# Where the recurrence's first estimates of h and x are kept: a change to a fused RNN, attention and feed-forward kernel

## The chip, the cores and the metric

The kernel runs on one core of one Trainium2 chip. Its time is the device time of one execution in microseconds; of the kernel before there are three runs without a profile (3483.38, 3485.22 and 3495.51 us, median 3485.22) and one execution with a profile. The engines are called as in the profile: PE is TensorE's matmul, PEld its weight load, DVE is VectorE, ACT is ScalarE, POOL is GpSimd, SP is SyncE. PSUM is eight banks of 512 fp32 numbers per partition; POOL cannot reach it.

## What is computed

The input is x of shape (8, 128, 128) and a condition of shape (8, 128). A recurrence of 128 steps comes first; a latent attention, a gated scan and six layers of local attention and feed-forward follow on its result. All is fp32. The change lies in the recurrence, which is

```python
xw = jnp.einsum('ntd,dh->nth', x, Wx) + b
def step(prev_h, xw_t):
    next_h = jnp.tanh(xw_t + prev_h @ Wh)
    return (next_h, next_h)
_, hs = jax.lax.scan(step, h0, jnp.swapaxes(xw, 0, 1))
```

with 8 sequences, a state of 128 numbers each, and h0 the condition. The rest of the program follows from `hs`.

## The kernel before

**One step.** The kernel forms `prev_h @ Wh` and `x_t @ Wx` not as one matmul each but as sums in a fixed order, number by number. For each of the 8 sequences (a "row" n here) and each output, it first needs the running sums over the 128 products. They come from a matmul of the weights with a triangle (the state times the matrix `upto`), 128 running sums per row; kept with 12 added or taken away (`OFFSET`) they are the *guess*. The error of each link is the *rest*: the guess shifted by one place, minus the guess itself, plus the exact product, and the product is built of four products of parts, upper and lower half of the weight's bits (`w_part`) times upper and lower half of the value (a diagonal matrix, `diag`), in fp32r. Rests, guesses and minus the guesses are laid side by side in one chain (`adds`, three numbers per link: rest, guess, minus guess; it lies in the tile `qkv_w`), and a sum over the chain (`fold`, L993, one instruction for 1 to 3 rows before) gives the row's result. The state's `tanh` follows on DVE as some forty small instructions and ends in `h_made`; `open_step` copies it (`h_now`, L969) and prepares the next step.

**Halves.** The 8 rows go in two halves of four rows; a half's sums fill one PSUM bank of 4 x 128. h's sums lie in banks 0 and 1, x's in bank 4. h's rests go in quarters of two rows (banks 2, 3, 0, 1), x's rests in halves through bank 6. x runs one step ahead: in step t the kernel makes x's sums and rests for t + 1.

**Who does what.** PE: the sums (L1355, L1303), identity matmuls that bring the difference of guesses into the rests' bank (L1322 for h; L1331 and, with minus the identity, L1332 for x), the products (L1298). ACT: the guess (`take_sums`, L705, PSUM to SBUF; h's guess in the tile `w1`, x's in `b1`), the diagonals of x (L698) and six of h's lower ones (L693), and the copies of the rests into the chain (`place_rests`, L716). DVE: h's difference of guesses (`difference_h`, L987, SBUF minus SBUF), the folds, the upper diagonals of h's first half (L980), `tanh`. POOL: the second half's triangle of h and both of x (L572), the upper diagonals of h's second half, the last lower ones, and the copies of guess and minus guess into the chain (`place_sums`, L581 and L583).

**What sets the order.** Each engine has its own program, written out by hand, with one loop over the 128 steps; an engine takes its instructions strictly in the order written, and semaphores with counts (`wait_ge`) tie the engines together. There is no planner. A wait therefore also holds all that is written behind it. The semaphores that matter: `sum_ready` (sums in PSUM), `guessed`, `diff_ready`, `split_h` (h's upper and lower parts), `rest_ready` (rests in PSUM), `rest_placed` and `sum_placed` (in the chain), `x_scanned` (x's folds done, so its chain may be overwritten).

## Time and profile before

| | |
|---|---|
| runs without a profile | 3483.38, 3485.22, 3495.51 us |
| the profiled execution | 3494.39 us, span 3492.2 us |
| granted TensorE clock over the span | 0.982 |
| busy, share of the span | PE 84%, DVE 83%, POOL 75%, ACT 69%, PEld 57% |
| instructions | 60815 |
| recurrence, 43 to 2150 us | 2107 us |

The span is the time from the first to the last instruction; the execution's own time lies 2.2 us around it. The busy share is a mean over the recurrence (43 to 2150 us), the latent attention and gate, and the layers, which have different limits. In the recurrence all steps look alike, so one step can stand for all. In a timeline row equal instructions that follow each other without a pause are merged; the second number is from the first start to the last end, and a bracket shows how long the engine stood idle before it and whose instruction ended that. Starts of successive instructions lie closer than their durations, since each overlaps the next a little; fp32 matmuls are recorded as two passes each.

### The profile page before, as it was taken

What the parts mean: (1) busy time and instruction counts of PE and PEld (TensorE: products, weight loads), DVE (VectorE), ACT (ScalarE), POOL (GpSimd) and SP (SyncE); (2) the same over time, 40 slices, a digit from 0 to 9 for tenths busy, and PEclk for the clock granted to TensorE, in tenths of its full rate; (3) what the DMA queues carried; (4) which work ended last, traced back from release to release, by engine and by line L of the source; (5) the groups of instructions that cost most, each with busy time, mean ns of one, the idle gap of its engine ahead of it and who ended that gap; (6) DMA issues with size and microseconds to landing.
All of it is one profiled execution on the core that took longest, in us unless ns stands there. A gap on an engine that the chain in (4) does not pass through costs nothing.

```text
span 3492.2 us, 60815 instructions
## 1 busy us (share of the span) xinstructions
PE 2949.2 (84%) x14887; PEld 2000.2 (57%) x14887; DVE 2899.3 (83%) x8319; ACT 2393.0 (69%) x5656; POOL 2607.6 (75%) x2800
## 2 busy tenths in 40 slices
PE   5888888888888888888888888978999999999997
PEld 3445445445545544544554555765777677777776
DVE  5999999999999999999999997336777877777775
ACT  5777777777777777777777775336666666666665
POOL 7888888888888887888888885008778777787773
PEclk9999999999999999999999998879999999999998
DMA  1000000000000000000000002000010101000000
GB/s 32 0 0 0 0 0 0 0 0 0 0 0 0 0 0 0 0 0 0 0 0 0 0 0 70 1 1 1 0 35 0 35 0 35 0 3 31 0 0 7
DMA packets 21861, 21.97 MB, mean 6 GB/s; under 512 B 6335, under 2 KB 19397, under 8 KB 21061
## 3 DMA queue, kind: packets, MB, share of 16 engines
q1 hardware_dynamic: 21828, 21.55, 1.9%
q8 instruction: 20, 0.33, 0.0%
q14 instruction: 13, 0.10, 0.0%
HBM read 21.02 MB, written 0.52 MB: 6 GB/s over the span
## 4 chain that ended last, share of the span: by engine, by line
PE 54%; DVE 16%; ACT 15%; issue 10%; POOL 3%; ACTq 1%; DVEq 0%; SPq 0%; DMA 0%; POOLq 0%
PE bank L1298 13%; PE bank L1322 8%; PE bank L1331 7%; PE bank L1332 6%; ACT diag_x L698 6%; ACT qkv_w L716 4%; PE bank L1303 3%; DVE rot_s L1211 3%; DVE qk L987 3%; PE bank L1549 3%; ACT w L705 2%; DVE rot_c L1211 2%; DVE ss L1214 2%; PE bank L1627 2%; PE bank L1601 2%
## 5 line engine op out<-in xcount | busy, mean ns | idle before, releaser
L993 DVE TENSOR_REDUCE bank<-qkv_w 128x2 f32<-128x766 f32 (+2 forms) x1024 | 925.3, 946 | 28.8 <-ACT qkv_w L716 28.8
L716 ACT COPY qkv_w<-bank 128x256 f32<-128x256 f32 (+1 forms) x770 | 480.0, 623 | 550.3 <-PE bank L1298 547.3
L698 ACT ACTIVATE diag_x<-eye,X 128x128 fp32r<-128x128 f32 x2072 | 630.5, 390 | 0.0
L1298 PE MATMUL bank<-diag_h,w_part 128*128 128x256 f32 x2048 | 495.5, 354 | 0.0
L581 POOL TENSOR_TENSOR qkv_w<-w,offset 128x512 f32<-128x512 f32 x256 | 331.3, 1294 | 156.8 <-ACT w L705 156.8
L1322 PE MATMUL bank<-qk,eye 128*128 128x256 f32 x1024 | 331.1, 405 | 98.0 <-DVE qk L987 98.0
L651 POOL TENSOR_TENSOR qk<-rot_c,rot_s 128x512 f32<-128x512 f32 x192 | 256.5, 1336 | 209.4 <-DVE rot_s L1211 209.4
L1331 PE MATMUL bank<-b,eye 128*128 128x512 f32 x516 | 277.8, 620 | 128.8 <-ACT qkv_w L716 128.8
L1298 PE MATMUL bank<-diag_x,w_part 128*128 128x512 f32 x1032 | 386.0, 495 | 0.0
L1298 PEld LDWEIGHTS bank<-diag_h,w_part 128*128 128x128 f32 x2048 | 335.0, 190 | 88.3 <-issue 61.2
L581 POOL TENSOR_TENSOR qkv_w<-b,offset 128x512 f32<-128x512 f32 x258 | 269.0, 1043 | 89.4 <-DVE bank L993 75.4
L658 POOL TENSOR_TENSOR rs<-rs,halfs 128x8 f32<-128x8 f32 x192 | 320.1, 1667 | 16.0
L987 DVE TENSOR_TENSOR qk<-w 128x512 f32<-128x512 f32 x256 | 225.3, 880 | 116.8 <-ACT w L705 116.8
L1549 PE MATMUL bank<-qkv_w,xsT 128*128 (+1 forms) x576 | 310.7, 622 | 8.8 <-DVE rot_s L1211 7.3
L1355 PE MATMUL bank<-qT,wh 128*128 128x256 f32 x512 | 144.6, 405 | 168.4 <-DVE qT L972 168.4
L583 POOL TENSOR_SCALAR qkv_w<-w 128x512 f32<-128x512 f32 x256 | 273.2, 1067 | 17.3
L1303 PE MATMUL bank<-kT,wx 128*128 128x512 f32 x516 | 265.6, 596 | 16.8 <-POOL kT L572 16.0
L1298 PEld LDWEIGHTS bank<-diag_x,w_part 128*128 128x128 f32 x1032 | 195.0, 189 | 147.2 <-issue 123.9
L572 POOL TENSOR_TENSOR kT<-upto,xT 128x512 f32<-128x512 f32 x260 | 265.0, 1040 | 10.3
L1332 PE MATMUL bank<-b,qk 128*128 128x512 f32 x516 | 264.3, 594 | 0.0
L693 ACT ACTIVATE diag_h<-eye,part 128x128 fp32r<-128x128 f32 x768 | 250.4, 394 | 0.0
L583 POOL TENSOR_SCALAR qkv_w<-b 128x512 f32<-128x512 f32 x258 | 229.2, 888 | 17.5
(235 smaller groups left out, 6883.8 us busy)
## 6 DMA issues: line engine op xcount, KB each, us to landing
qkv_w<-in_L_ffn_Wqkv SPq DMA_DIRECT2D x6, 1536.0 KB
o_w<-in_L_ffn_Wo SPq DMA_DIRECT2D x6, 512.0 KB
w<-in_L_ffn_W SPq DMA_DIRECT2D x6, 341.0 KB
b<-in_L_ffn_b SPq DMA_DIRECT2D x6, 341.0 KB
w<-in_L_ffn_W SPq DMA_DIRECT2D x6, 128.0 KB
x_tok<-in_x SPq DMA_DIRECT2D x1, 512.0 KB
masks<-in_masks SPq DMA_DIRECT2D x1, 512.0 KB, 3.5
out<-o_fin SPq DMA_DIRECT2D x1, 512.0 KB, 3.2
```

Source lines behind the costliest of these rows:

```text
L581: pool.tensor_tensor(adds[n][:, rows, :, 1], src, offset[:, 0:1].unsqueeze(2).to_broadcast([P, 4, D]), ALU.add)
L583: ins = pool.tensor_scalar(adds[n][:, rows, :, 2], src, -1.0, OFFSET, ALU.mult, ALU.add)
L698: ins = act.activation(diag[1][:, d, m, :], eye[:], ACT.Copy, scale=scale)
L716: act.copy(adds[n][:, rows, :, 0], src).then_inc(rest_placed[n], 1)
L987: dve.tensor_tensor(diff_h[:, rows, :], guess[0][:, rows, 0:D], guess[0][:, rows, 1:], ALU.subtract).then_inc(diff_ready, 1)
L993: return dve.tensor_reduce((sum_h, sum_x)[n][:, a:b], chain[n][:, a:b, 0:LINKS], AX_X, ALU.add)
L1298: return pe.matmul(dst, w_part[:, n, w], diag[n][:, d, a:b, :].rearrange("p n k -> p (n k)"), start=start, stop=stop)
L1303: pe.matmul(bank[:, SUM_BANK_X if n else half, :], (wh, wx)[n][:], tri[n][:, 4 * half:4 * half + 4, :].rearrange("p n k -> p (n k)"), star ...
L1322: pe.matmul(bank[:, bnk, 0:(b - a) * D], eye[:], diff_h[:, a:b, :].rearrange("p n k -> p (n k)"), start=False, stop=False)
L1331: pe.matmul(rows, eye[:], guess[1][:, a:b, 0:D], start=True, stop=False)
L1332: pe.matmul(rows, minus_eye, guess[1][:, a:b, 1:], start=False, stop=False)
L1549: pe.matmul(bank[:, c % 2, :], xsT[:, par, :], w[:, at:at + BANK], start=True, stop=True).then_inc(qkv_ready, 1)
```

## The change

h's sums now start from a bank that PE has filled with 12 by a small bf16 matmul of a row of ones with a row of twelves (`offset_h`, two banks per step), and are added onto it; so the guess is what stands in PSUM, and it is not copied to SBUF as such. ACT writes it, less 12, straight into the chain (`place_guess_h`), and later minus the guess for the first half (`place_minus_h`); POOL writes minus the guess for the second half from the chain. DVE forms the difference from the PSUM bank (shifted by one) and the chain's guess and writes it into the rests' bank (`difference_h`), where PE adds the products: h's identity matmuls go. h's rests are now in halves (banks 2 and 3), each product 512 wide.

For x, ACT writes minus the guess into the rests' bank (`less_guess_x`), and PE adds the shifted guess with one identity matmul; the one with minus the identity goes. x's lower diagonals move from ACT to POOL, h's upper diagonals of the first half from DVE to POOL, all of h's lower ones of the second half to POOL (of the first half: ACT). x's folds are two of four rows, one before and one behind both differences. One matmul per rests' bank is added ahead of the loop.

```diff
+            def offset_h():
+                for half in range(2):
+                    pe.matmul(bank[:, half, :], offset16[:, 0:D], offset16[:, D:], start=True, stop=True,
+                              skip_group_check=True)
 ...
             def rests_x(half, count):
-                pe.wait_ge(guessed[1], count)
-                pe.matmul(rows, eye[:], guess[1][:, a:b, 0:D], start=True, stop=False)
-                pe.matmul(rows, minus_eye, guess[1][:, a:b, 1:], start=False, stop=False)
-                pe.wait_ge(diag_x_ready, count)
-                times(at, 1, 0, 0, a, b, False, False)
-                other_products(1, REST_BANK_X, a, b)
+                pe.wait_ge(less_guess, count)
+                pe.matmul(rows, eye[:], guess_x[:, a:b, 0:D], start=False, stop=True, skip_group_check=True)
+                for d in range(2):
+                    pe.wait_ge(diag_x_ready[d], count)
+                    times(at, 1, 0, d, a, b, False, False)
+                    ins = times(at, 1, 1, d, a, b, False, d == 1)
+                ins.then_inc(rest_ready[1], 1)
 ...
+            def less_guess_x(half):
+                act.activation(bank[:, REST_BANK_X, :], guess_x[:, 4 * half:4 * half + 4, 1:], ACT.Copy,
+                               scale=-1.0).then_inc(less_guess, 1)
+            def place_guess_h(half, count):
+                act.wait_ge(sum_ready[0], count)
+                act.activation(adds[0][:, 4 * half:4 * half + 4, :, 1], bank[:, half, :].rearrange("p (n k) -> p n k", k=D),
+                               ACT.Identity, bias=offset[:, 0:1], scale=1.0).then_inc(guess_placed, 1)
+            def place_minus_h(count):
+                act.wait_ge(diff_ready, count)
+                act.activation(adds[0][:, 0:4, :, 2], bank[:, 0, :].rearrange("p (n k) -> p n k", k=D),
+                               ACT.Identity, bias=offset[:, 1:2], scale=-1.0).then_inc(minus_placed[0], 1)
 ...
-            def difference_h(half, halves):
-                rows = slice(4 * half, 4 * half + 4)
-                dve.wait_ge(guessed[0], halves)
-                dve.tensor_tensor(diff_h[:, rows, :],
-                                  guess[0][:, rows, 0:D], guess[0][:, rows, 1:],
-                                  ALU.subtract).then_inc(diff_ready, 1)
+            def difference_h(half, count):
+                sums_ = bank[:, half, :].rearrange("p (n k) -> p n k", k=D)
+                dst = bank[:, REST_BANKS_H[half], :].rearrange("p (n k) -> p n k", k=D)
+                placed = adds[0][:, 4 * half:4 * half + 4, :, 1]
+                dve.wait_ge(guess_placed, count)
+                dve.tensor_scalar(dst[:, :, 0:1], sums_[:, :, 0:1], -1.0, OFFSET, ALU.mult, ALU.add)
+                dve.scalar_tensor_tensor(out=dst[:, :, 1:], in0=sums_[:, :, 0:D - 1], scalar=-OFFSET, in1=placed[:, :, 1:],
+                                         op0=ALU.add, op1=ALU.subtract).then_inc(diff_ready, 1)
 ...
+                pool.wait_ge(split_h, this)
+                for half in range(2):
+                    diagonal(0, 0, half, part[:, 0, 4 * half:4 * half + 4], diag_upper_h)
+                pool.tensor_copy(hT[:, bass.ds(t, 1), :].rearrange("p a n -> p (a n)"), h_now[:]).then_inc(h_ready, 1)
+                diagonal(0, 1, 1, part[:, 1, 4:8], diag_lower_h[1])
+                pool.wait_ge(guess_placed, counts[1])
+                pool.tensor_tensor(adds[0][:, 4:8, :, 2], adds[0][:, 4:8, :, 1],
+                                   signs[:, 1:2].unsqueeze(2).to_broadcast([P, 4, D]), ALU.mult).then_inc(minus_placed[1], 1)
+                pool.wait_ge(rest_ready[1], counts[1])
+                diagonal(1, 1, 1, lower_x(around, 1), diag_x_ready[1])
                 pool.wait_ge(x_scanned, this)
+                place_sums_x(0, counts[2])
+                place_sums_x(1, counts[3])
+                pool.wait_ge(rest_ready[1], counts[2])
+                diagonal(1, 1, 0, lower_x(beyond, 0), diag_x_ready[1])
                 for half in range(2):
                     triangle(1, at_step(value(pool, t + 2)), half, tri_x)
```

The instructions' order shows three places. First ACT from the start of the loop body; `w` is h's guess before, `b` x's guess, `qkv_w` the chain. Before:

```order
L693 ACTIVATE diag_h<-eye,part 128x128 [waits split_h]
L693 ACTIVATE diag_h<-eye,part 128x128
L704 ISA
L705 ACTIVATE w<-bank,offset 128x4x128 [waits sum_h]
L704 REGISTER_ALU
L705 ACTIVATE w<-bank,offset 128x4x128 [waits sum_h]
L693 ACTIVATE diag_h<-eye,part 128x128 x4
L704 REGISTER_ALU [waits sum_placed_x]
L705 ACTIVATE b<-bank,offset 128x4x128 [waits sum_x]
L713 ISA
L716 COPY qkv_w<-bank 128x256 [waits rest_h]
L713 REGISTER_ALU
```

After (L735 is the guess into the chain, L741 minus the guess, L753 the rests, L728 x's guess, L723 minus the guess into PSUM):

```order
L735 ACTIVATE qkv_w<-bank,offset 128x512 [waits sum_h]
L777 REGISTER_ALU
L712 ACTIVATE diag_h<-eye,part 128x128 [waits split_h]
L712 ACTIVATE diag_h<-eye,part 128x128 x3
L741 ACTIVATE qkv_w<-bank,offset 128x512 [waits diff_h]
L753 COPY qkv_w<-bank 128x256 [waits rest_h]
L753 COPY qkv_w<-bank 128x256
L727 REGISTER_ALU [waits sum_placed_x]
L728 ACTIVATE b<-bank,offset 128x4x128 [waits sum_x]
L723 ACTIVATE bank<-b 128x512 [waits rest_placed_x,guessed_x]
L753 COPY qkv_w<-bank 128x256 [waits rest_h]
L753 COPY qkv_w<-bank 128x256
```

h's guess stood behind two diagonals of h; two writes into the chain now come first, of which the first stands just ahead of this piece, all four diagonals behind them, and x's guess and its minus stand between the second and the third copy of h's rests.

PE from h's products on; `qk` is the tile of h's difference before. Before:

```order
L1298 MATMUL bank<-diag_h,w_part 128x256 [waits diag_upper_h]
L1298 MATMUL bank<-diag_h,w_part 128x256
L1373 ISA [waits diff_h]
L1322 MATMUL bank<-qk,eye 128x256 [waits diag_lower_h]
L1298 MATMUL bank<-diag_h,w_part 128x256 x3
L1373 REGISTER_ALU
L1322 MATMUL bank<-qk,eye 128x256 [waits diag_lower_h]
L1298 MATMUL bank<-diag_h,w_part 128x256 x3
L1298 MATMUL bank<-diag_h,w_part 128x256 [waits guessed_h,diag_second_h]
L1298 MATMUL bank<-diag_h,w_part 128x256
```

After:

```order
L1340 MATMUL bank<-diag_h,w_part 128x512 [waits diag_upper_h,diff_h]
L1340 MATMUL bank<-diag_h,w_part 128x512
L1340 MATMUL bank<-diag_h,w_part 128x512 [waits diag_upper_h,diff_h]
L1340 MATMUL bank<-diag_h,w_part 128x512
L1340 MATMUL bank<-diag_h,w_part 128x512 [waits diag_lower_h0]
L1340 MATMUL bank<-diag_h,w_part 128x512
L1340 MATMUL bank<-diag_h,w_part 128x512 [waits diag_lower_h1]
L1340 MATMUL bank<-diag_h,w_part 128x512
L1344 REGISTER_ALU [waits guessed_x]
L1345 MATMUL bank<-kT,wx 128x512 [waits tri_x]
L1364 MATMUL bank<-b,eye 128x512 [waits less_guess_x,rest_placed_x]
```

The identity matmuls (L1322) are gone, the products are twice as wide and half as many; both halves' upper products come ahead of the lower ones, and x's identity matmul (L1364) waits for ACT's write into the bank.

DVE from x's first fold on. Before:

```order
L993 TENSOR_REDUCE bank<-qkv_w 128x2 [waits sum_placed_x,rest_placed_x]
L986 REGISTER_ALU
L987 TENSOR_TENSOR qk<-w 128x512 [waits guessed_h]
L993 TENSOR_REDUCE bank<-qkv_w 128x1
L987 TENSOR_TENSOR qk<-w 128x512 [waits guessed_h]
L993 TENSOR_REDUCE bank<-qkv_w 128x3
L1096 ISA
L993 TENSOR_REDUCE bank<-qkv_w 128x2 [waits sum_placed_h,rest_placed_h]
```

After:

```order
L1035 TENSOR_REDUCE bank<-qkv_w 128x4 [waits sum_placed_x,rest_placed_x]
L1029 TENSOR_SCALAR bank<-bank 128x4 [waits guess_placed_h]
L1030 SCALAR_TENSOR_TENSOR bank<-bank,qkv_w 128x4x127
L1028 REGISTER_ALU
L1029 TENSOR_SCALAR bank<-bank 128x4 [waits guess_placed_h]
L1030 SCALAR_TENSOR_TENSOR bank<-bank,qkv_w 128x4x127
L1035 TENSOR_REDUCE bank<-qkv_w 128x4 [waits sum_placed_x,rest_placed_x]
L1138 ISA
L1140 REGISTER_ALU [waits rest_placed_h]
L1035 TENSOR_REDUCE bank<-qkv_w 128x2 [waits minus_placed_h0]
```

The four rows of x that were split over three folds around the differences now stand as one fold ahead of them, and x's last rows, which came behind h's fourth row, ahead of h's first; each difference is two instructions, of which the first writes four numbers.

## Rows read from the trace of the kernel before

**Rows 1.** The page: busy time, share, instructions; granted clock in 40 slices.
```profile
PE 2949.2 (84%) x14887; PEld 2000.2 (57%) x14887; DVE 2899.3 (83%) x8319; ACT 2393.0 (69%) x5656; POOL 2607.6 (75%) x2800
...
PEclk9999999999999999999999998879999999999998
```

**Rows 2.** Busy time by stretch; this one is the recurrence.
```profile
43.00:2150.00 2107.00, 1712.07 (x6394) 1060.86 (x6393) 1967.77 (x6649) 1563.22 (x4093) 1708.61 (x1789) 1.00 0.00 0
```

**Rows 3.** Waits in the recurrence: total us, times, longest us.
```profile
ACT qkv_w L716 <- PE bank L1298: 534.0, 505, 3.0
...
DVE qk L987 <- ACT w L705: 114.3, 127, 1.7
```

**Rows 4.** Timeline of ScalarE, one step: start us, us, instruction, count, idle before.
```profile
1013.77 0.83 ACT L716 COPY qkv_w<-bank 128x512 f32<-128x512 f32 x1 [3.00 <-PE bank L1298]
1014.45 2.43 ACT L698 ACTIVATE diag_x<-eye,X 128x128 fp32r<-128x128 f32 x8
1016.79 0.68 ACT L693 ACTIVATE diag_h<-eye,part 128x128 fp32r<-128x128 f32 x2
1017.37 1.24 ACT L705 ACTIVATE w<-bank,offset 128x512 f32<-128x512 f32 x2
...
1030.23 0.83 ACT L716 COPY qkv_w<-bank 128x512 f32<-128x512 f32 x1 [3.00 <-PE bank L1298]
```

**Rows 5.** Timeline of VectorE in the same step.
```profile
1014.52 0.17 DVE L969 COPY h_now<-bank 128x8 f32<-128x8 f32 x1
...
1015.54 0.68 DVE L980 TENSOR_TENSOR diag_h<-eye,bank 128x512 fp32r<-128x512 f32 x1
1016.23 0.96 DVE L993 TENSOR_REDUCE bank<-qkv_w 128x2 f32<-128x766 f32 x1
1018.08 0.69 DVE L987 TENSOR_TENSOR qk<-w 128x512 f32<-128x512 f32 x1 [0.89 <-ACT w L705]
...
1020.14 4.77 DVE L993 TENSOR_REDUCE bank<-qkv_w 128x3 f32<-128x1149 f32 x5
...
1024.96 0.94 DVE L993 TENSOR_REDUCE bank<-qkv_w 128x2 f32<-128x766 f32 x1
```

**Rows 6.** Timeline of TensorE in the same step.
```profile
1015.07 1.13 PE L1355 MATMUL bank<-qT,wh 128*128 128x256 f32 x4 [1.34 <-DVE qT L972]
...
1027.28 1.13 PE L1331 MATMUL bank<-b,eye 128*128 128x512 f32 x2 [1.00 <-ACT qkv_w L716]
1028.24 1.02 PE L1332 MATMUL bank<-b,qk 128*128 128x512 f32 x2
1028.70 1.49 PE L1298 MATMUL bank<-diag_x,w_part 128*128 128x512 f32 x4
```

**Rows 7.** Groups by line and form: busy us, mean ns, idle before.
```profile
L993 DVE TENSOR_REDUCE bank<-qkv_w 128x3 f32<-128x1149 f32 x128 | 172.1, 1345 | 0.0
...
L1017 DVE TENSOR_TENSOR_SCAN bank<-bank,f_add 128x96 f32<-128x96 f32 x128 | 45.3, 354 | 0.0
...
L716 ACT COPY qkv_w<-bank 128x256 f32<-128x256 f32 x512 | 262.0, 512 | 133.0 <-PE bank L1298 130.0
...
L716 ACT COPY qkv_w<-bank 128x512 f32<-128x512 f32 x258 | 218.0, 845 | 417.3 <-PE bank L1298 417.3
...
L705 ACT ACTIVATE w<-bank,offset 128x512 f32<-128x512 f32 x256 | 159.2, 672 | 0.0
...
L854 ACT COPY probT<-bank 128x512 f32<-128x512 f32 x192 | 102.9, 594 | 1.8 <-PE bank L1397 1.8
...
L572 POOL TENSOR_TENSOR kT<-upto,xT 128x512 f32<-128x512 f32 x260 | 265.0, 1040 | 10.3
```

**Rows 8.** Line L928: duration ns min/median/max, first and last start.
```profile
L928 DVE COPY xT<-bank x1: 1078/1078/1078, 6.8 to 6.8; 128x512 f32<-128x512 f32 x1
```

**Rows 9.** TensorE's timeline in the layers.
```profile
2410.14 0.33 PE L1658 MATMUL bank<-eye,xn 128*128 128x128 f32 x1 [1.90 <-DVE xn L1274]
```

**Rows 10.** Busy time by stretch just after, PEclk the granted clock.
```profile
2412.00:2419.00 7.00, 6.47 (x30) 4.36 (x31) 6.40 (x9) 2.24 (x4) 5.09 (x5) 0.52 0.01 2
```

More of the change, by code:

```diff
@@ L263, in program @@
         quot_part = sb("quot_part", [P, NB, 2])
-        clamped, rc, q0, nq, small_x, h_upper = (own(0, NB) for _ in range(6))
+        clamped, rc, q0, nq, small_x = (own(0, NB) for _ in range(5))
         q_tmp = sb("q_tmp", [P, 4, NB])
@@ L536, in _ @@
                     pool.memset(rest_seq[:, 3 * block_ + r::9, 3:4], c_low)
-            for n in range(2):
-                ins = pool.memset(guess[n][:, :, 0:1], OFFSET)
-            ins.then_inc(rnn_const, 1)
+            pool.memset(guess_x[:, :, 0:1], OFFSET).then_inc(rnn_const, 1)
             pool.memset(wd[:], 0.0)
@@ L599, in _ @@
                 counts = [value(pool, two + n) for n in (1, 2, 3, 4)]
+                around, beyond = (value(pool, (t + n) % T) for n in (1, 2))
                 pool.wait_ge(h_static, this)
@@ L702, in take_sums, with lower_h @@
-            def take_sums(n, half, count):
-                act.wait_ge(sum_ready[n], count)
-                act.activation(guess[n][:, 4 * half:4 * half + 4, 1:],
-                               bank[:, SUM_BANK_X if n else half, :].rearrange("p (n k) -> p n k", k=D), ACT.Identity,
-                               bias=offset[:, 1:2], scale=1.0).then_inc(guessed[n], 1)
-            def place_rests(n, counts, first, last):
-                rows_ = NB // len(counts)
-                for m in range(first, last):
-                    act.wait_ge(rest_ready[n], counts[m])
-                    rows = slice(rows_ * m, rows_ * m + rows_)
-                    src = bank[:, REST_BANK_X if n else REST_BANKS_H[m], 0:rows_ * D].rearrange("p (n i) -> p n i", n=rows_)
-                    act.copy(adds[n][:, rows, :, 0], src).then_inc(rest_placed[n], 1)
+            def lower_h():
+                for n in range(4):
+                    ins = act.activation(diag[0][:, 1, n, :], eye[:], ACT.Copy, scale=part[:, 1, n:n + 1])
+                ins.then_inc(diag_lower_h[0], 1)
@@ L718, in _, with place_rests_h @@
+            def place_rests_h(half, count):
+                act.wait_ge(rest_ready[0], count)
+                for m in range(2):
+                    rows = slice(4 * half + 2 * m, 4 * half + 2 * m + 2)
+                    act.copy(adds[0][:, rows, :, 0],
+                             bank[:, REST_BANKS_H[half], 2 * m * D:2 * m * D + 2 * D].rearrange(
+                                 "p (n i) -> p n i", i=D)).then_inc(rest_placed[0], 1)
             act.wait_ge(in_x, 64)
@@ L1097, in placed_h @@
                     if m % 2 == 0:
-                        dve.wait_ge(sum_placed[0], counts[m // 2])
+                        dve.wait_ge(minus_placed[m // 2], this)
                 dve.sem_clear(rnn_op)
+                placed_x(counts[0])
+                fold(1, 0, 4)
+                for half in range(2):
+                    difference_h(half, counts[half])
                 placed_x(counts[1])
-                for half in range(2):
-                    fold(1, *X_SCAN[half])
-                    difference_h(half, counts[half])
-                fold(1, *X_SCAN[2])
+                fold(1, 4, 8).then_inc(x_scanned, 1)
                 placed_h(0)
@@ L1109, in _ @@
                 fold(0, 2, 4)
-                fold(1, *X_SCAN[3]).then_inc(x_scanned, 1)
+                dve.wait_ge(x_scanned, this)
+                step(dve.tensor_scalar(xw[:], sum_x, rnn_b[:], None, ALU.add))
                 placed_h(2)
                 fold(0, 4, 6)
-                dve.wait_ge(x_scanned, this)
-                step(dve.tensor_scalar(xw[:], sum_x, rnn_b[:], None, ALU.add))
                 placed_h(3)
```

204 lines of the change are left out of this document (103 added, 101 removed).

## The prediction

> **What bounds the kernel now.** I read the page first, for busy shares and clock. PE and DVE are both busy over 80% of the span and the clock is at 2.4 GHz nearly throughout [rows 1], so neither names the bound. The sum by stages comes next: the recurrence takes 2107 of 3492 us, and the change touches nothing else but a few setup instructions [rows 2]. In it DVE is busy 1968 us, PE 1712, POOL 1709, ACT 1563; no one is full. The list of waits shows who stands still: ACT waits 534 us for PE's rests and DVE 114 us for h's guess [rows 3].
>
> So the timeline of one step has to be followed, from h_now at 1014.52. The period is the distance of equal rows: 1013.77 to 1030.23 on ACT, 16.46 us [rows 4]; 128 of them are 2107 us, the whole stage. What the reader is to see is a ring through ACT's queue. PE ends x's second rests [rows 6], ACT copies them (1013.77), must then write eight diagonals of x (2.43 us) and two of h, and only at 1017.37 does it turn h's first sums into the guess, although PE had begun those sums at 1015.07 and they last 1.13 us [rows 4, 6]. DVE idles 0.89 us for it, subtracts at 1018.08 and from there has no gap until the last fold at 1024.96 [rows 5]. PE starts x's second rests at 1027.28 after ACT's copy of the first and needs 1.02 us for each fp32 matmul (spaced 0.86, as 1027.28, 1028.24 and 1028.70 show with the 0.1 of a restart), then 1.49 for four products [rows 6], and the ring closes at 1030.23. Behind it runs a second ring, DVE's own: it is 1.1 us shorter, since the sums are ready at about 1016.20 and the guess is begun 1.17 later. Whoever shortens the first ring by more meets DVE.
>
> **The change, part by part, in us per step after h_now.** The stretch from the last fold to the next h_now is not touched: 16.46 - 10.44 = 6.02 us (10.44 is 1024.96 - 1014.52) [rows 5]. So the question is when the last fold starts.
>
> First ring. For x, four diagonals instead of eight stand on ACT in each group (2.43 for eight of them is 0.29 apart [rows 4], so 1.17 less), the two minus-identity matmuls leave PE (2 x 0.86), and x's second copy now comes last in ACT's step with nothing between it and h's sums. Placed one after the other (with the times found below: h's fourth copy done at 8.97, x's guess to 9.54, four diagonals to 10.71, x's first copy 0.85, minus the guess 0.75 with its waits, PE 0.10 + 0.86 + 0.94 + 0.16, to 14.37, x's second copy 0.85) it ends at 15.2 to 15.3, and h's next sums are ready 1.7 after the next h_now: this ring has some 2 us of room and no longer bounds.
>
> DVE's ring. *Start.* diag_h leaves DVE (0.68 [rows 5]) and goes to POOL. What stands behind it is the loop's turn (branch, semaphore clear), which it covered. Bounds 0 and 0.68; I take 0.06, first fold at 1.65 instead of 1.71, because the loop's turn is also in the queue. *Fold of four rows of x.* Three rows last 1.345, two 0.96, so 0.40 per row; spaced 1.66 [rows 5, 7]: to 3.31. The guess of the first half is placed by then: sums 1.7, ACT's strided write 0.67 + 0.25 = 0.92 (the contiguous form is 0.672, and a copy into the same every-third-number layout costs 0.845 against 0.594 [rows 7]) gives 2.65. So DVE's wait of 0.89 is gone; 0.66 of cover is left.
>
> *The two subtractions,* now PSUM minus SBUF into PSUM, one number in three read from the chain. No row shows one. Lower bound: the present subtraction, 0.69 [rows 5]. Upper bound: the scan, 0.354 for 96 numbers; less 0.15 fixed (h_now's eight numbers last 0.17) 2.1 ns each, so 508 take 1.23 [rows 5, 7]. In between lies the stride: ACT's 0.25 extra over 512 is 0.5 ns per number, hence 1.32 instead of 0.83, and 1.32 x 512 + 0.15 = 0.83; a DVE copy that writes every eighth number lasts 1.078 [rows 7, 8]. I take 0.83, spaced 0.75, since ACT's layout is this one. With a small instruction of 0.08 ahead of each, the second ends at 3.31 + 0.08 + 0.75 + 0.08 + 0.83 = 5.05.
>
> The Trainium skill (SBUF — State Buffer, under "Door 1: The DMA port swizzle") has a rule that speaks against this edit: accesses in the same 16-byte line run at full speed, each crossing pays, so every third fp32 pays on most numbers. The trace agrees for writes (0.845 against 0.594); no row shows a read. If reads pay as writes do, the sum stands; if not, the subtraction is 0.69 and the time 35 us lower.
>
> *PE.* Upper products of the second half, then the lower ones of the first: the four products of rows 6 run 0.23 apart (from 1028.24 + 0.86 to 1030.19, less 0.16 until the last is written), so 0.05 + 4 x 0.235 + 0.17: rest 1 is ready at 6.20. The identity matmuls for h and 16 products of 256 are replaced by eight of 512, the same 1.9 us; the fp32 identity (0.43 x 4) is gone from the path. *ACT behind it:* two copies of 256 (0.37 apart), x's guess (0.57, 0.15 more until it may read its own result), minus the guess into PSUM, then the third copy, 0.51 [rows 7]. ACT writing PSUM has no row: bounds 0.59 (contiguous copy) and 1.07 (strided by eight) for its duration; I take 0.65, 0.55 apart, nearest the contiguous rows, as both sides are contiguous. 6.25 + 0.74 + 0.72 + 0.55 + 0.51 = 8.77. DVE is ready for the third h fold at 4.96 + 1.66 = 6.62, waits for the first copy until 6.80, then 2 x 0.86 + 0.13 = 8.65, waits to 8.80, and begins the last fold at 9.66.
>
> *Sum:* 10.44 - 9.66 = 0.78 earlier, 128 times: 100 us. The new period is 15.68. x's pipeline ends before the next h_now, on ACT at 15.3 and on POOL at 14.9 (from x's first guess at 7.7 seven writes of at most 1.04 [rows 7]; in all thirteen and a small copy, near the 1709 / 128 = 13.35 of now [rows 2]): hidden; if POOL's cover goes, each step grows by what it overruns, as its first job is h's second triangle. The hT copy and the lower diagonal now stand behind two diagonals of POOL instead of one, and the second half's minus copy behind them; of these the diagonal is ready at 4.5 and asked for by PE at 6.0, the minus copy at 5.5 and asked for by DVE at 8.7. The other new waits are reached after their event: ACT's minus copy (behind it the copies of the rests) at 4.6, the first subtraction ends at 4.2; POOL's last x diagonal (behind it the triangles) at 11.9, the rests are ready at 10.6; PE's offsets at 10.4, the minus copy is done at 5.5. The two offset matmuls (0.44) lie between x's rests, where PE waits. Setup: three more fp32 matmuls (2.6 us) and two more POOL diagonals (2.0) before the first step, eight ACT diagonals less: +2. The profiled execution took 3494.4 for a span of 3492.2, so it would be 3396; it is 9 above the median of the runs, 3485.2, and against that the forecast is 3387.
>
> **Rivals.** *A, the stride costs as much as in the DVE copy, 1.07 [rows 8].* Two subtractions each 0.24 later and a PE restart: +0.58, period 16.25, 3460. For it: that row is DVE's own. Against: it strides by eight, not three.
>
> *B, slower: the fused two-operation subtraction out of and into PSUM runs far below one number per cycle.* Place: both instructions on DVE, everything behind them. The gain of 0.78 pays for 2 x 0.34 beyond 0.83, so the point is 1.2 us each. At 1.5 the last fold starts at 9.66 + 1.34 + 0.1 = 11.1, period 17.1, 3570. For it: the scan's 2.1 ns, which gives 1.23 with no stride. Against: the triangle and the diagonal, PSUM times SBUF, run at 1.05 ns (0.68 for 512 [rows 5]).
>
> *C, the clock.* PE loses 3.0 us of work per step net and gains a pause: from 14.4 to 16.2, 1.9 us, where before it was about 1.3 (last product to 1015.07) at a held 2.4 GHz. In the layers a pause of 1.90 before 2410.14 was followed by a stretch with a granted clock of 0.52, that is 1.2 GHz mostly [rows 9, 10]. If the products behind the subtraction run at 1.2 GHz in every step, 0.94 is added: period 16.6, 3505. Against: there the matmuls around were narrow, here they are full. In most phases only the sums are hit, and 0.66 covers them: +0.2, 3410. The Trainium skill (TensorE: Matmul & The Clock Gate, under "A second HAM failure mode: psum-queue depth-cycling") says that short idles between groups can make the clock swing; the trace shows swings in the layers and none in the recurrence. By it the time would be this rival's.
>
> *D, ACT's write to PSUM costs 1.0:* +0.35, one to one, as it stands before the third copy: 3432. I count it with the forecast.
>
> **How the numbers follow.** Forecast with D 0.56, range of its own 3345 to 3435 (unstrided subtraction to D); A 0.15; B 0.15; C at its worst 0.08; another wait that eats the gain 0.06, half of it within 0.5%. A measurement of this kernel tells about 0.5% from no change, 17 us, so 3468 and 3503 are the limits. Faster: 0.56 and 0.14 of A = 0.70; within: 0.01 of A, 0.02 of B, 0.03 of C, 0.03 of the last = 0.09; slower: 0.13 of B, 0.05 of C, 0.03 of the last = 0.21. The range 3345 to 3500 leaves out B and the tail of C above, little below.
>
> **What would show it.** Period 15.7 between equal ACT rows; no DVE gap ahead of the first subtraction; each 0.8 us; DVE gaps of 0.1 to 0.2 ahead of the first and third h fold, released by ACT's copies; POOL's writes all 1.04; ACT idle ahead of h's first sums, where it was full; granted clock 1.0 in the recurrence. It would be wrong with a subtraction over 1.0, a row of minus the guess near 1.0, a clock below 1.0 there, or POOL reaching h's triangle late.

## The result and the profile after

| | before | after |
|---|---|---|
| four runs, median (range) | 3484.4 us (3483.38 to 3495.51) | 3387.68 us (3386.6 to 3388.72) |
| ratio after to before, 95% interval | | 0.9715 (0.9695 to 0.9735) |
| profiled execution, span | 3494.39, 3492.2 us | 3387.04, 3385.2 us |
| one step of the recurrence | 16.46 us | 15.67 us |

The forecast was 3387, with a range of 3345 to 3500. The fourth run of the kernel before, 3483.58, was taken beside those of the changed kernel, whose four runs include the profiled one. In all periods below, a step is the distance between two copies to h_now, as a mean over the recurrence without its first step.

The page after, which answers to [rows 1], and the busy time by stretch, which answers to [rows 2]. The columns of the second are PE, PEld, DVE, ACT, POOL, then the granted clock:

```profile
PE 2591.3 (77%) x12477; PEld 1621.5 (48%) x12587; DVE 2810.1 (83%) x8061; ACT 2325.5 (69%) x4750; POOL 2593.7 (77%) x2804
...
PEclk9999999999999999999999998979999999999998
```

```profile
43.00:2050.00 2007.00, 1371.79 (x4097) 686.64 (x4096) 1879.51 (x6399) 1500.44 (x3205) 1693.84 (x1793) 1.00 0.00 0
```

The share of DVE is 83% on both pages, and the kernel is 97 us faster: a busy share says nothing here, since work and waiting fell together. DVE's busy time is 1967.77 of 2107 us before and 1879.51 of 2007 after, that is 15.37 and 14.67 us per step. In the list of waits of the recurrence the 114 us for h's guess [rows 3] are gone, 0.90 per step; two others stand there, 0.76 together:

```profile
DVE bank L1035 <- issue: 64.9, 127, 0.6
...
DVE bank L1035 <- ACT qkv_w L753: 31.9, 127, 0.3
```

By this account most of the gain looks like work taken off DVE, above all the diagonal of 0.68. The run a_hdve below shows that it is not.

ScalarE's timeline, one step, against [rows 4]. L735 is h's guess into the chain, L741 minus the guess, L753 the copies of h's rests, L746 those of x's:

```profile
1012.34 0.85 ACT L746 COPY qkv_w<-bank 128x512 f32<-128x512 f32 x1 [1.01 <-PE bank L1340]
1015.24 1.81 ACT L735 ACTIVATE qkv_w<-bank,offset 128x512 f32<-128x512 f32 x2 [2.06 <-PE bank L1355]
1016.89 1.25 ACT L712 ACTIVATE diag_h<-eye,part 128x128 fp32r<-128x128 f32 x4
1018.04 0.94 ACT L741 ACTIVATE qkv_w<-bank,offset 128x512 f32<-128x512 f32 x1
1019.82 0.84 ACT L753 COPY qkv_w<-bank 128x256 f32<-128x256 f32 x2 [0.84 <-PE bank L1340]
...
1021.21 0.60 ACT L723 ACTIVATE bank<-b 128x512 f32<-128x512 f32 x1
1021.75 0.88 ACT L753 COPY qkv_w<-bank 128x256 f32<-128x256 f32 x2
...
1028.01 0.84 ACT L746 COPY qkv_w<-bank 128x512 f32<-128x512 f32 x1 [1.01 <-PE bank L1340]
```

Where ACT was full between x's last copy and h's guess, it now stands idle for 2.06 us: the first ring no longer bounds. VectorE in the same step, against [rows 5]; h_now is at 1013.52:

```profile
1013.52 0.17 DVE L1013 COPY h_now<-bank 128x8 f32<-128x8 f32 x1
...
1015.14 1.76 DVE L1035 TENSOR_REDUCE bank<-qkv_w 128x4 f32<-128x1532 f32 x1 [0.51 <-issue]
1016.80 0.16 DVE L1029 TENSOR_SCALAR bank<-bank 128x4 f32<-128x4 f32 x1
1016.87 0.84 DVE L1030 SCALAR_TENSOR_TENSOR bank<-bank,qkv_w 128x508 f32<-128x508 f32 x1
1017.61 0.17 DVE L1029 TENSOR_SCALAR bank<-bank 128x4 f32<-128x4 f32 x1
1017.68 0.85 DVE L1030 SCALAR_TENSOR_TENSOR bank<-bank,qkv_w 128x508 f32<-128x508 f32 x1
1018.43 1.75 DVE L1035 TENSOR_REDUCE bank<-qkv_w 128x4 f32<-128x1532 f32 x1
1020.44 1.82 DVE L1035 TENSOR_REDUCE bank<-qkv_w 128x2 f32<-128x766 f32 x2 [0.25 <-ACT qkv_w L753]
```

No wait stands ahead of the first subtraction. Two small ones are new: 0.51 ahead of x's first fold, which no instruction of another engine ends ("issue"), and 0.25 for ACT's copy of h's rests. TensorE's pause ahead of h's sums, against [rows 6]:

```profile
1026.48 1.50 PE L1340 MATMUL bank<-diag_x,w_part 128*128 128x512 f32 x4
1029.75 1.56 PE L1355 MATMUL bank<-qT,wh 128*128 128x256 f32 x5 [1.77 <-DVE qT L1016]
```

### The profile page after: what moved, and what is told of

It reads as the page before. It is cut to its first block, busy times and chain, and to the rows that moved or that the text cites. A ratio compares the mean times of both kernels' runs of the same rounds, so it can differ in the third digit from the quotient of the medians.

```text
span 3385.2 us, 53537 instructions
## 1 busy us (share of the span) xinstructions
PE 2591.3 (77%) x12477; PEld 1621.5 (48%) x12587; DVE 2810.1 (83%) x8061; ACT 2325.5 (69%) x4750; POOL 2593.7 (77%) x2804
## 4 chain that ended last, share of the span: by engine, by line
DVE 53%; PE 21%; issue 16%; ACT 4%; POOL 3%; DVEq 2%; SPq 0%; DMA 0%; POOLq 0%; ACTq 0%
DVE bank L1035 12%; PE bank L1340 5%; DVE bank L1030 3%; DVE bank L1007 3%; DVE rot_s L1253 3%; DVE sq L1007 3%; DVE rot_c L1253 3%; DVE ss L1256 3%; PE bank L1582 2%; DVE qT L1016 2%; PE bank L1660 2%; DVE fix_trace L1101 2%; PE bank L1444 2%; PE bank L1634 2%; ACT qkv_w L753 2%
## 5 line engine op out<-in xcount | busy, mean ns | idle before, releaser
L1035 DVE TENSOR_REDUCE bank<-qkv_w 128x2 f32<-128x766 f32 (+1 forms) x768 | 914.0, 1220 | 123.6 <-issue 64.9
L1355 PE MATMUL bank<-qT,wh 128*128 128x256 f32 (+1 forms) x768 | 254.6, 467 | 224.0 <-DVE qT L1016 224.0
L669 POOL TENSOR_TENSOR qk<-rot_c,rot_s 128x512 f32<-128x512 f32 x192 | 256.9, 1338 | 207.8 <-DVE rot_s L1253 207.8
L735 ACT ACTIVATE qkv_w<-bank,offset 128x512 f32<-128x512 f32 x256 | 232.0, 960 | 261.1 <-PE bank L1355 261.1
L1340 PE MATMUL bank<-diag_h,w_part 128*128 128x512 f32 x1024 | 307.4, 422 | 118.1 <-DVE bank L1030 106.9
L587 POOL TENSOR_TENSOR diag_h<-eye,part 128x512 fp32r<-128x512 f32 x384 | 394.0, 1040 | 0.0
L1364 PE MATMUL bank<-b,eye 128*128 128x512 f32 x516 | 273.3, 611 | 156.7 <-ACT bank L723 156.7
L718 ACT ACTIVATE diag_x<-eye,X 128x128 fp32r<-128x128 f32 x1036 | 328.0, 389 | 0.3 <-DVE X L1128 0.3
L1340 PEld LDWEIGHTS bank<-diag_h,w_part 128*128 128x128 f32 x1024 | 172.7, 188 | 302.8 <-DVE bank L1030 279.8
L746 ACT COPY qkv_w<-bank 128x512 f32<-128x512 f32 x258 | 217.3, 842 | 134.6 <-PE bank L1340 133.4
L753 ACT COPY qkv_w<-bank 128x256 f32<-128x256 f32 x512 | 218.4, 508 | 104.3 <-PE bank L1340 104.3
L587 POOL TENSOR_TENSOR diag_x<-eye,X 128x512 fp32r<-128x512 f32 x259 | 269.7, 1041 | 10.2
```

The lines of the kernel that those rows point to most:

```text
L587: pool.tensor_tensor(diag[n][:, d, rows, :], eye[:].unsqueeze(1).to_broadcast([P, 4, D]), values.unsqueeze(2).to_broadcast([P, 4, D]), ALU ...
L718: ins = act.activation(diag[1][:, 0, m, :], eye[:], ACT.Copy, scale=scale)
L753: act.copy(adds[0][:, rows, :, 0], bank[:, REST_BANKS_H[half], 2 * m * D:2 * m * D + 2 * D].rearrange("p (n i) -> p n i", i=D)).then_inc(r ...
L1035: return dve.tensor_reduce((sum_h, sum_x)[n][:, a:b], chain[n][:, a:b, 0:LINKS], AX_X, ALU.add)
L1340: return pe.matmul(dst, w_part[:, n, w], diag[n][:, d, a:b, :].rearrange("p n k -> p (n k)"), start=start, stop=True, skip_group_check=True)
L1355: return pe.matmul(bank[:, half, (a - 4 * half) * D:(b - 4 * half) * D], wh[:], tri[0][:, a:b, :].rearrange("p n k -> p (n k)"), start=Fal ...
```

## The experiments

The kernel before was run again beside each group of experiments; its medians lie between 3484 and 3489 us, and each ratio is to the one taken beside the run. b_psum and a_contig compute with other numbers than the right ones (said with each): they measure a cost and are not kernels to be used.

| run | us, median | ratio to before, 95% | step, us |
|---|---|---|---|
| before | 3484 to 3489 | | 16.46 |
| after | 3387.7 | 0.9695 to 0.9735 | 15.67 |
| b_swap | 3431.3 | 0.9817 to 0.9853 | 16.03 |
| b_psum | 3311.2 | 0.9475 to 0.9506 | 15.07 |
| a_xboth | 3383.9 | 0.969 to 0.9725 | 15.65 |
| a_hdve | 3394.2 | 0.9714 to 0.9746 | 15.74 |
| a_contig | 3346.5 | 0.9571 to 0.9609 | 15.36 |
| a_order | 3375.0 | 0.9657 to 0.969 | 15.61 |
| o_mm | 3333.7 | 0.955 to 0.9603 | 15.31 |
| a_rot | 3318.8 | 0.9496 to 0.9531 | 15.15 |
| f_mm | 3275.6 | 0.937 to 0.9401 | 14.81 |
| f_both | 3277.2 | 0.9371 to 0.941 | 14.81 |
| h1_flat | 3262.8 | 0.9343 to 0.9392 | 14.72 |
| h2_late | 3239.6 | 0.9275 to 0.9301 | 14.47 |

**b_swap: was it ACT's order alone?** On the kernel before:

```diff
-                place_rests(1, counts[2:4], 0, 2)
+                place_rests(1, counts[2:4], 0, 1)
                 diagonals_x(beyond, 0, 0)
                 diagonals_x(beyond, 0, 1)
+                place_rests(1, counts[2:4], 1, 2)
```

> The kernel before, with one edit: ACT writes x's eight diagonals for the next group ahead of x's second copy of the rests, while it would wait 3.0 us for PE anyway. My theory: the bound was ACT's order alone, 2.43 us of diagonals between the copy and h's first guess; with them in ACT's pause DVE no longer waits 0.89 for the guess, DVE's own ring (1968 us of work in 128 steps, 15.4 each) takes over, period 15.5 to 15.6 instead of 16.46, time 3365 to 3380, as much as the whole change gave (3388). Rival one: what counted is the work taken off ACT and PE for x (four diagonals, the minus-identity matmul); the order alone then only shifts the wait to x's second copy, which stands ahead of h's diagonals still, gain under 0.3 per step, 3450 or more. Rival two: PE's pause ahead of h's sums grows and its clock falls: 3450 to 3500 and a granted clock under 1.0 in the recurrence.

Measured 3431, period 16.03: a gain of 0.43 per step where 0.86 to 0.96 was expected. DVE's wait for the guess is gone, as expected, but its two differences (L988 here) have grown, and so has a write of POOL. The two engines' timelines:

```profile
1022.95 1.50 DVE L988 TENSOR_TENSOR qk<-w 128x512 f32<-128x512 f32 x1
...
1024.83 0.81 DVE L988 TENSOR_TENSOR qk<-w 128x512 f32<-128x512 f32 x1
```

```profile
1022.86 1.04 POOL L581 TENSOR_TENSOR qkv_w<-w,offset 128x512 f32<-128x512 f32 x1
1023.97 1.24 POOL L583 TENSOR_SCALAR qkv_w<-w 128x512 f32<-128x512 f32 x1
```

POOL's first write ends at 1023.90, the difference that started beside it at 1024.45, 0.55 later, as if most of its 0.69 had only begun then. POOL's next write, 0.90 elsewhere, lasts 1.24. The second rival is out (the clock is 1.00 in the recurrence), and the first put the time at 3450 or more, with a gain under 0.3; the theory of one bound, moved away, is incomplete.

**b_psum: is it the two engines' SBUF traffic?** On top of b_swap:

```diff
-                                  guess[0][:, rows, 0:D], guess[0][:, rows, 1:],
+                                  guess[0][:, rows, 0:D], bank[:, half, :].rearrange("p (n k) -> p n k", k=D),
...
                         pe.wait_ge(guessed[0], counts[1])
+                        pe.wait_ge(diff_ready, counts[1])
```

> The kernel before with the diagonals moved (as in b_swap, 3431) and one more edit: h's difference reads minus the guess from h's sums in PSUM instead of SBUF (the result is off by a constant, and PE's products of the third and fourth quarter wait for the second difference, since they overwrite those banks). My theory: in b_swap the two differences last 1.50 and 0.81 us instead of 0.69 each, since an instruction of DVE with two SBUF inputs and POOL's guess writes stand in each other's way (each difference there ends 0.55 behind the end of POOL's write); with one input in PSUM both last 0.69 to 0.75, period 15.3 to 15.6, 3345 to 3375. Rival: the 1.50 is ACT's guess not being there yet; then the first difference stays at 1.5 and the time at 3431 or above.

The sums in PSUM lack the 12 that the guess has, so the rests are other numbers. Measured 3311, below the expected range. The differences' group before, in b_swap and here:

```profile
L987 DVE TENSOR_TENSOR qk<-w 128x512 f32<-128x512 f32 x242 | 213.0, 880 | 108.9 <-ACT w L705 108.9
```

```profile
L988 DVE TENSOR_TENSOR qk<-w 128x512 f32<-128x512 f32 x248 | 286.7, 1156 | 0.0
```

```profile
L988 DVE TENSOR_TENSOR qk<-w,bank 128x512 f32<-128x512 f32 x245 | 165.9, 677 | 0.0
```

With one input in PSUM a difference lasts 0.68 in every step, though it lies wholly inside one of POOL's writes of the guess, and those are back at 1.04 and 0.90: 2 x (1.156 - 0.677) is 0.96, and the period fell by 0.96. DVE now has no pause over 0.15 us in a step. The kernel before has the same collision, 0.38 per step, in the second of its differences:

```profile
1019.15 1.07 DVE L987 TENSOR_TENSOR qk<-w 128x512 f32<-128x512 f32 x1
```

```profile
1018.12 1.55 POOL L581 TENSOR_TENSOR qkv_w<-w,offset 128x512 f32<-128x512 f32 x1 [1.19 <-ACT w L705]
```

Here too the difference ends (1020.22) 0.55 behind POOL's write (1019.67), which itself takes 1.55 instead of 1.04. It looked like plain work without a gap. The Trainium skill (SBUF — State Buffer, under "SBUF: two separate sides") says that a DVE instruction with two SBUF inputs and a GpSimd instruction that reads SBUF lock each other out for a whole instruction. The trace agrees: the difference that reads SBUF twice ends 0.55 behind POOL's write, and the one that reads PSUM runs beside it.

**a_xboth: what is x's part worth?** The changed kernel with x's old matmuls and all of x's diagonals on ACT:

```diff
-                pe.wait_ge(less_guess, count)
-                pe.matmul(rows, eye[:], guess_x[:, a:b, 0:D], start=False, ...)
+                pe.wait_ge(guessed, count)
+                pe.matmul(rows, eye[:], guess_x[:, a:b, 0:D], start=True, ...)
+                pe.matmul(rows, minus_eye, guess_x[:, a:b, 1:], start=False, ...)
```

> The changed kernel with x's part undone but its place in the order kept: x's eight diagonals of a group all on ACT, and PE adds guess and minus guess by two identity matmuls instead of ACT writing minus the guess into the bank. My theory: x's ring had about 1.5 us of room in the changed kernel (copy ends 15.34 after h_now, h's guess begins at 17.4); it grows by about 1.3 us and still ends before h's next sums, so 3385 to 3395, no difference, with ACT's idle time ahead of h's guess down from 2.06 to about 0.8. Rival: x's part was what paid; then x's copy stands in front of h's guess again and the time goes to 3430 or more.

Measured 3383.9, just under what was expected and 0.1% from the changed kernel: with the new order kept, x's part is worth nothing. ACT waits 0.80 instead of 2.06 ahead of h's guess, as expected:

```profile
1014.08 1.81 ACT L728 ACTIVATE qkv_w<-bank,offset 128x512 f32<-128x512 f32 x2 [0.80 <-PE bank L1338]
```

**a_hdve: what is the diagonal's move worth?** DVE writes `diag[0][:, 0, 0:4, :]` behind `split_h` again, from upper parts that one more small instruction makes, and POOL does not.

> The changed kernel with the upper diagonals of h's first half written by DVE again (0.68) ahead of the loop's turn, as in the kernel before, and not by POOL. My theory: the loop's turn (0.51 idle after the move) hides behind that diagonal, so the move was worth 0.1 only, 1.71 instead of 1.62 to x's first fold: period 15.7 to 15.8, 3393 to 3402. Rival: the turn comes on top of the diagonal, and the move was worth 0.68: 3470.

Measured 3394.2 and 0.07 per step, at the lower end. The fold follows the diagonal without a pause, 1.70 us behind h_now (1016.77 here), where the changed kernel has 1.62:

```profile
1017.79 0.69 DVE L1024 TENSOR_TENSOR diag_h<-eye,bank 128x512 fp32r<-128x512 f32 x1
1018.47 1.76 DVE L1040 TENSOR_REDUCE bank<-qkv_w 128x4 f32<-128x1532 f32 x1
```

Of the 0.68 us taken off DVE 0.61 came back, 0.51 of it as the pause ahead of the fold. Against the kernel before, DVE here is as busy, 15.31 us per step (1926.75 of 1980) and 15.38 there (1850.40 of 1980), and the step is 0.72 shorter: nearly all that the change gains, it gains in DVE's waiting.

**a_rot: is "issue" the loop's turn?** On DVE alone:

```diff
                 dve.sem_clear(rnn_op)
-                placed_x(counts[0])
-                fold(1, 0, 4)
...
                 open_step(value(dve, t + 2))
+                placed_x(counts[2])
+                fold(1, 0, 4).then_inc(x_first, 1)
```

> The changed kernel, DVE's program alone: the loop's boundary is put behind x's first fold of four rows (1.76 us) instead of ahead of it, so that the loop's turn (0.51 idle ahead of that fold) is covered. My theory: DVE's ring bounds, so all behind the fold moves up by 0.4 to 0.5; but h's first rests then wait for ACT's minus copy (queue: guess to 17.05, four diagonals to 18.14, minus to 18.98), which gives back nothing of it as DVE asks at 19.8; PE's order keeps the wait of 0.25. Period 15.2 to 15.3, 3335. Rival one: the idle time is the semaphore's or the write's settling and not the loop's turn; then nothing moves, 3388. Rival two: PE's clock, if its pause ahead of the sums passes 1.9.

Measured 3318.8 and 0.52 per step: all of the 0.51, and more than I expected. The fold now follows `part` at once, and the loop's turn (semaphore clear and branch) runs beside it:

```profile
1027.03 0.17 DVE L1023 TENSOR_TENSOR part<-bank,part 128x8 f32<-128x8 f32 x1
1027.19 1.76 DVE L1037 TENSOR_REDUCE bank<-qkv_w 128x4 f32<-128x1532 f32 x1
```

**a_contig: is it the stride?**

```diff
-                dve.scalar_tensor_tensor(..., in1=placed[:, :, 1:],
+                dve.scalar_tensor_tensor(..., in1=guess_x[:, 4 * half:4 * half + 4, 2:],
```

> The changed kernel with the second input of h's subtraction read from x's guess, 127 numbers side by side per row, instead of from the chain, one number in three (the rests of h, and so the result, are other numbers). The stride theory of the prediction: 0.84 falls to 0.69, the last fold comes 0.3 earlier, 3350. Rival: what makes it 0.84 is the access to PSUM or the second operation; then 0.84 stays and so does 3388.

It takes x's guess in the place of h's. Measured 3346.5 (two runs), 41 us less; the subtraction lasts 0.684, so the stride costs 0.15 on each, and 0.684 for 508 numbers against the 0.677 of b_psum's plain difference for 512 leaves next to nothing for the second operation and the write into PSUM:

```profile
L1030 DVE SCALAR_TENSOR_TENSOR bank<-bank,b 128x508 f32<-128x508 f32 x240 | 161.5, 684 | 0.0
```

**a_order and o_mm: the wait of 0.25, and the clock.** In a_order PE finishes the first half before it starts the second:

```diff
                     for w in range(2):
                         times(bank[:, REST_BANKS_H[half], :], 0, w, 0, 4 * half, 4 * half + 4, False, False)
-                for half in range(2):
                     pe.wait_ge(diag_lower_h[half], this)
```

> The changed kernel, PE's order of h's products: upper and lower products of the first half, then those of the second, instead of both upper ones first. The second subtraction ends at 1018.53, so the first half's rests would be ready 0.9 us earlier (1018.9), and DVE's wait of 0.25 ahead of h's first fold goes: period 15.43, 3356 if only this counts. Rival, the clock: x's work on ACT and PE moves up by up to 0.9 while h_now moves by 0.25, so PE's pause ahead of h's sums grows from 1.77 to 2.3 or 2.4; if a pause over 1.9 brings the clock to 1.2 GHz here as it did in the layers, h's sums and products run at half speed in every step, 0.8 to 1.0 more per step, 3440 to 3490, granted clock 0.5 to 0.7 in the recurrence.

Measured 3375.0, between the two. The mean step of 15.61 is none of the usual ones: the short ones are 15.3, and 40 of 127 are over 15.8. Before one of these, TensorE's timeline and the granted clock (last but two) around it:

```profile
1009.60 3.14 PE L1355 MATMUL bank<-qT,wh 128*128 128x256 f32 x6 [2.21 <-DVE qT L1016]
```

```profile
1008.00:1010.00 2.00, 0.40 (x2) 0.37 (x3) 1.90 (x14) 0.27 (x1) 0.70 (x1) 1.00 0.00 0
1010.00:1012.00 2.00, 2.00 (x6) 1.28 (x5) 1.49 (x2) 0.93 (x1) 2.00 (x3) 0.57 0.00 0
1012.00:1014.00 2.00, 2.00 (x4) 0.71 (x4) 1.48 (x5) 1.25 (x4) 1.67 (x4) 0.57 0.00 0
1014.00:1016.00 2.00, 1.74 (x8) 1.12 (x7) 2.00 (x2) 2.00 (x6) 2.00 (x2) 1.00 0.00 0
```

```profile
1013.75 0.17 DVE L1029 TENSOR_SCALAR bank<-bank 128x4 f32<-128x4 f32 x1 [0.53 <-ACT qkv_w L735]
```

After a pause of 2.21 the clock is at 1.2 GHz for most of 4 us, the six matmuls take 3.14 instead of the 1.99 that they take in the changed kernel, and DVE waits 0.53 for h's second guess. The longer step makes the next pause 1.75, the clock holds, and it starts over. Of the 127 pauses, 75 last 2.18 to 2.24 us, and 52 of these are followed by a fall; the other 52 last 1.74 to 1.78, and none is. o_mm gives PE its second identity matmul for x back, which shortens the pause, and takes the write of minus the guess off ACT:

> a_order (PE's order of h's products alone, 3375, clock 0.95 in the recurrence) with x's rests made by two identity matmuls of PE again. PE thereby does 1.7 us more fp32 work per step and its pause ahead of h's sums falls from 2.2 to about 1.0 to 1.7. The clock theory: nothing else in a_order kept the gain back, so the clock is 1.00 in the recurrence, the period 15.43 in every step and the time 3350 to 3358. Rival: the order of the products moves another wait; then this kernel stays at 3375 or goes above it, since PE has more to do.

Measured 3333.7 at a clock of 1.00, with a pause of 1.23:

```profile
1021.01 1.99 PE L1345 MATMUL bank<-qT,wh 128*128 128x256 f32 x6 [1.23 <-DVE qT L1006]
```

A kernel in which TensorE has 1.7 us more to do in a step is 41 us faster. That ACT has less to do is not the reason: a_order's own short steps are 15.3 too, with ACT's write in place. The step is also 0.12 better than I expected: DVE's wait of 0.25 costs another 0.1, since an instruction behind a wait doesn't overlap the end of the one before it. From x's second fold to h's first it is 2.01 us in the changed kernel (1018.43 to 1020.44), and 1.67 in a_order.

**f_mm, f_both: together.** f_mm is a_rot, a_order and o_mm in one; f_both adds x's lower diagonals on ACT.

> The changed kernel with three edits: DVE's loop boundary behind x's first fold (as a_rot, 3319), PE's order of h's products (as a_order, 3375), and x's rests by two identity matmuls of PE with no write of minus the guess by ACT (one half of a_xboth, where x's part was worth nothing). My theory: a_order lost its gain to PE's clock, which fell after pauses of 2.22 us ahead of h's sums; the two fp32 matmuls make x's ring 0.4 to 0.6 us longer, so the pause is 1.6 to 1.8 again and the clock holds, DVE's wait of 0.26 ahead of h's first fold is gone as well: period 14.9, 3285 to 3295. Rival one: the pause passes 1.9 all the same, clock under 0.98 in the recurrence, 3300 to 3320. Rival two: x's ring now bounds, period over 15.1.

> As f_mm, and x's lower diagonals on ACT as well, so that x's part is wholly that of before. My theory: x's ring grows by another 0.7 us, had 0.8 in a_xboth and gets about as much back from the earlier rests of h while the period shrinks by 0.75: ACT reaches h's guess with 0.2 to 0.7 idle, PE's pause is 0.6 to 1.1, the clock holds, same time as f_mm, 3285 to 3300. Rival: ACT is late for h's guess again, as in the kernel before; the time grows one for one from there, 3310 or more.

Measured 3275.6 and 3277.2, equal, and both some 10 us below what was expected: with a step of 14.81 the half of x's part in which they differ is worth nothing still.

**h1_flat, h2_late: the stride taken out.** From f_both (two of ACT's diagonals of h also come ahead of the guess):

```diff
-                act.activation(adds[0][:, 4 * half:4 * half + 4, :, 1], bank[:, half, :]..., bias=offset[:, 0:1], ...)
+                act.activation(guess_h[:, 4 * half:4 * half + 4, :], bank[:, half, :]..., bias=offset[:, 0:1], ...)
...
+                act.copy(adds[0][:, 4:8, :, 1], guess_h[:, 4:8, :]).then_inc(in_chain[1], 1)
...
+                pool.tensor_tensor(adds[0][:, 0:4, :, 1], guess_h[:, 0:4, :], signs[:, 0:1]..., ALU.mult)...
```

> f_both (3277) with the stride taken out of DVE's reading: ACT writes h's guess side by side into a tile of its own (0.67 us instead of 0.96), DVE subtracts from that (a_contig showed 0.68 instead of 0.84), POOL puts the first half into the chain (one more write of 1.04) and ACT the second; two of ACT's diagonals of h come ahead of the guess, in its idle time. My theory: DVE's ring bounds and nothing takes its place, so both subtractions give 0.15 each: period 14.6, 3235 to 3250. Rival: ACT's queue, which has one more copy (0.9) ahead of minus the guess, or POOL's, which places the guess 5.4 us after h_now at the earliest where DVE now asks at 5.8, makes DVE wait ahead of h's first fold; then the gain is under 15 us, or there is a loss.

Measured 3262.8, 14 us less where 27 to 42 were expected: the rival, in its milder form. h2_late moves the `act.copy` behind the first two copies of h's rests:

> h1_flat (3263) with ACT's copy of the second half's guess into the chain moved behind the first two copies of h's rests. In h1_flat the subtractions took 0.27 less per step and the period fell by 0.10 only; DVE starts h's first fold 0.11 us late there, for ACT's copy of the rests, which stands behind that guess copy (0.87). My theory: ACT reaches the rests' copy 0.5 earlier, the wait goes and no other comes, since DVE asks for the moved copy at 7.7 us and has it at 6.4: period 14.58 to 14.62, 3247 to 3253. Rival: x's guess, 0.6 later now, or the third copy makes the fold of h's second half late: 3263 or more.

Measured 3239.6, below the expected range: 0.9288 of before (0.9275 to 0.9301), 4.4% below the changed kernel. The lateness of 0.11 in h1_flat was worth 0.21, for the lost overlap as above: from x's second fold to h's first it is 1.87 us there and 1.66 here. In its recurrence DVE goes from the second subtraction to the third fold without a pause:

```profile
1016.31 0.68 DVE L1024 SCALAR_TENSOR_TENSOR bank<-bank,w 128x508 f32<-128x508 f32 x1
1016.90 3.46 DVE L1029 TENSOR_REDUCE bank<-qkv_w 128x4 f32<-128x1532 f32 x3
```

## Why the prediction was right, and where its account was not

**The sum.** The last fold was to start 9.66 us after h_now. The last two folds are one row of VectorE's timeline:

```profile
1022.30 1.82 DVE L1035 TENSOR_REDUCE bank<-qkv_w 128x2 f32<-128x766 f32 x2
```

It ends at 1024.12 and one fold lasts 0.95, so the last starts at 1023.17, which is 9.65 after h_now. The step fell by 0.79 where 0.78 was forecast. That the whole time agrees to 0.7 us is luck: the four runs before lie 12 us apart, the first step, with the setup, is 1.3 us shorter than before where the setup was to add 2, and the part behind the recurrence, which the change doesn't touch, took 1342 us in one profiled execution and 1338 in the other.

**DVE's start.** First fold at 1.65 forecast, 1.62 measured; a_hdve gives the diagonal's move 0.07 where the sum had 0.06. The reason given, that the loop's turn stands in the queue behind it, is what a_rot shows.

**The subtractions.** 0.83 forecast, 0.84 measured; the second ends at 5.01, forecast 5.05. The price was put down to the stride, between bounds of 0.69 and 1.23 us, and a_contig confirms it: 0.15 per instruction, 41 us for the kernel where the prediction gave 35. The rule of the Trainium skill on 16-byte lines (SBUF — State Buffer, under "Door 1: The DMA port swizzle") was weighed for this. The trace agrees with it for this read, 0.837 against 0.684, as it did for ACT's write.

**PE and ACT behind.** The first copy of h's rests starts at 6.30 (forecast 6.25), minus the guess into PSUM lasts 0.60 (forecast 0.65), the third copy ends some 0.5 after 1021.75, 8.7 (forecast 8.77). DVE waits for the first copy as expected, 0.25 for 0.18, and starts h's first fold at 6.92 where the sum had 6.80. The wait of 0.15 ahead of the third h fold does not appear, since DVE comes there that much later: two misses that cancel. POOL's last x triangle ends at 14.9 and x's second copy at 15.3, as forecast, though not all writes of POOL last 1.04: minus the guess takes 1.21.

**The rivals.** A, B and D are decided by the three rows named: 0.84, 0.60, no subtraction near 1.2. C was a real mechanism that missed by little: PE's pause was put at 1.9 and is 1.77, the clock held in all of the recurrence, and a_order shows the fall at 2.2.

**What the account had wrong.** It said that the second ring, DVE's own, is 1.1 us shorter than the first, as if the first could be cut alone. b_swap cuts the first alone and gains 0.43. The part of the account that failed is the plain 0.69 taken for the present difference: the first instruction lasts that, the second 1.07, and when the guess comes early both run into POOL's writes and take 2.31 together. It did no harm to the number, since the changed kernel's ring was added up from its own pieces, and the subtraction out of PSUM doesn't collide; but it hid where the gain is from. By the experiments: ACT's order alone is worth 0.43; a difference that reads PSUM is worth 0.96 more; that is 15.07, and the change reaches 15.67, since it exposes the loop's turn (0.51), reads with a stride (0.30), issues two small instructions (2 x 0.07) and waits for a copy (0.36), against the diagonal that it takes off DVE (0.68): 0.63 together, 0.60 measured. These are differences between other kernels and needn't add up so well. That h's identity matmuls leave PE was not tried alone; b_psum still has them, and DVE has no pause over 0.15 us there, so they cost nothing in it. And x's part, the half of the change that takes four diagonals of each group off ACT and an fp32 matmul off PE, is worth nothing once the order has moved (a_xboth). That ring had 2 us of room in my own sum, which says as much, but the prediction never drew that conclusion.

## What to carry to other kernels

Add up the new critical ring from its own rows and trust it over the list of what was removed: here work taken off an engine with room was worth nothing, and it cost 41 us where it lengthened TensorE's pause from 1.2 to 2.2 us. Before a kernel is rebuilt, look for the engine that idles just ahead of what it should have done already: one reordered line gave 56 us here, and a loop boundary put behind a long instruction 69 us. Where equal instructions last differently, look for what runs beside them: here the 0.38 us of a collision looked like plain work.

## What the runs showed of the hardware that was not expected

- A VectorE subtraction of 512 numbers with both inputs in SBUF lasts 0.69 when it begins ahead of GpSimd's write, and 0.81, 1.07 or 1.50 when it begins behind one; GpSimd's instructions, which read SBUF too, grow from 0.90 to 1.24 and from 1.04 to 1.55 (before, b_swap). With one input in PSUM it lasts 0.68 beside the same writes (b_psum).
- The changed kernel's pauses of TensorE, 1.75 to 1.78 us, did not lower the clock in any step; of 75 pauses of 2.18 to 2.24 in a_order, 52 were followed by a fall, of 52 of 1.74 to 1.78 none.
- A wait of 0.25 us on VectorE costs 0.36 per step (15.67 against o_mm's 15.31), 0.34 of it between the starts of the two folds, as the instruction behind the wait no longer overlaps the one ahead; one of 0.11 costs 0.21 (h1_flat against h2_late).
- A fused subtraction (two operations, 508 numbers, PSUM minus SBUF into PSUM) lasts 0.684 in a_contig, a plain one of 512 numbers with one input in PSUM 0.677 in b_psum; reading every third number of SBUF adds 0.15.
